# Value bias folded into the projection's bias, VectorE's chains in steps, and sixteen-bit transposes moved from TensorE to DMA

## The chip, the cores and the metric

The kernel runs on one core of a Trainium2 chip. The core has TensorE (PE, which has a second row for its weight loads), VectorE (DVE), ScalarE (ACT), GpSimd (POOL) and SyncE (SP, which here does nothing but issue DMAs), each with its own instruction queue worked off in order, and 16 DMA engines. Engines wait for each other through semaphores. The metric is the time of one execution on the device in microseconds, as a median.

## The reference, cut to what matters

Sixty-four sequences of 128 tokens with 128 features pass through four layers, each on a layer-normalised input and added to its input. The second operand of the two attentions is a context of 120 tokens.

```
def _L0_xattn_ref(x, ctx, Wq, bq, Wkv, bkv, Wproj, bproj, gq, gk):
    q = rms_norm((x @ Wq + bq).reshape(B, S, 16, 8), gq).transpose(0, 2, 1, 3)
    kv = (ctx @ Wkv + bkv).reshape(B, Sc, 2, 16, 8)
    k = rms_norm(kv[:, :, 0], gk).transpose(0, 2, 1, 3)
    v = kv[:, :, 1].transpose(0, 2, 1, 3)
    attn = softmax(einsum('bhsd,bhtd->bhst', q, k) / sqrt(8))
    out = einsum('bhst,bhtd->bhsd', attn, v) ...
    return out @ Wproj + bproj

def _L0_ffn_ref(x, w1, conv_w, conv_b, w2):          # 128 -> 512 -> 128
    h = silu(depthwise_conv1d(bit_linear(x, w1), conv_w, conv_b))
    return bit_linear(h, w2)                          # activations rounded to integers of -128..127 per row

x = x + _L0_xattn_ref(_layernorm(x), ctx, ...)
x = x + _L0_ffn_ref(_layernorm(x), ...)
x = x + _L1_xattn_ref(_layernorm(x), ctx, ...)        # one head of width 128
x = x + _L1_ffn_ref(_layernorm(x), ...)               # 8 experts of width 256; every token weighted by its gate
```

A row of `attn` sums to one, so a bias on the values comes out of the attention unchanged: `(attn @ (v + b)) @ Wproj + bproj` is `(attn @ v) @ Wproj + (b @ Wproj + bproj)`.

## The kernel before

The 64 sequences are cut into 16 groups of 4 (`GB`). A group passes through five stages: N (first layer norm, projections of Q, K and V, the RMS norms), A (attention of 16 heads, output projection), B (quantised feed-forward with the convolution), D (second attention, last layer norm, gate) and C (experts). They form a software pipeline: in one period stage N works on group i, A on i-1, B on i-2, D on i-3 and C on i-4. Twelve of the periods have all five stages; before them four fill the pipeline, and four empty it behind them.

Inside a period the order on each engine is a string of the table `TURNS`, one letter a step: the engine takes the next step of stage n, a, b, d or c as the string says. The stages' step lists are `n_steps` to `c_steps`. SP alone has its order written out, in its `body`.

The places that the change touches:

- Stage N, step `qkv`: V's projection lands in PSUM, and VectorE adds the bias `bv_s` in four instructions into `v_st` (L1037). Step `rms`: a chain of small VectorE instructions (`rsqrt`, L956 to L962), each of which waits for the one before it by a semaphore (`Chain.link`). Step `qkht`: TensorE transposes `q_hi` and `k_hi` (L492, L495), and ScalarE copies both to `qkht` (L745). From K's part SP issues 16 small DMAs, one a head, into the block-diagonal `kbd` (L413), after the last `max` step of the group ahead.
- Stage A: step `max` (L508) multiplies Q with `kbd` for four heads, VectorE takes the maxima (L1073); 16 such steps a group share one PSUM bank. Step `stacks` (four a group) transposes Q's stack (L518) and K's stack (L520) on TensorE, and ScalarE copies both to `st_t` (L752). `scores` (L532) multiplies them, ScalarE takes the exponentials (L756), `values` is L543.
- Stage B: step `quant` rounds the normalised input to integers (L1098 to L1107). Step `h2t` (four a group) transposes the hidden activations back (L590), VectorE finds each row's scale by a chain of four instructions (L1131 to L1134), ScalarE rounds (`hr`, L780); step `hit` transposes the integers on TensorE (L596) and ScalarE copies them from PSUM (L784); both steps use PSUM bank `pb`. `fc2` (L603) needs all four; L1136 forms its scales.
- Stage C: 16 units of three half-precision matmuls for `pg`, three for `pu`, and four for `py` (L697).

## Time and profile before

| | |
|---|---|
| median of 3 runs | 1278.15 us (1277.8 to 1279.9) |
| profiled execution | 1278.19 us |
| its span, first to last instruction | 1276.3 us |
| busy: PE, DVE, ACT, POOL | 1156.3, 1044.5, 865.6, 699.2 us |
| share of the span | 91%, 82%, 68%, 55% |
| mean granted TensorE clock | 0.951 of full |
| queue q1 (SP's DMAs): share of 16 engines' span | 8.4% |

Busy time counts stretches in which at least one instruction of the engine runs. TensorE's matmuls overlap: the next one starts before the one ahead has ended, so a group's array time is better read from the distance between starts. "Idle before" is time in which an engine stood still ahead of the group's instructions, with what released it. A row of stretches gives its bounds, its length, then the busy time of PE, PEld, DVE, ACT and POOL with the number of instructions in brackets, the granted TensorE clock as a share of full, the DMA engines' mean busy share and GB/s. SPq is the time that SP's queue spends to issue a DMA.

### The profile page before, as it was taken

How to read it: one execution, taken by the hardware profiler on the slowest of the kernel's cores; microseconds unless marked ns; L12 is line 12 of the kernel's file. 1: busy time of each engine (PE TensorE's matmuls, PEld its weight loads, DVE VectorE, ACT ScalarE, POOL GpSimd, SP SyncE). 2: the span in 40 equal slices, each digit the busy share in tenths (PEclk: the TensorE clock that was granted, in tenths of full speed). 3: DMA queues.
4: the chain of work that ended last, by engine and by line, in shares of the span. 5: the costliest groups of instructions: out<-in, count | busy, mean ns of one | idle time of the engine just before them, and what ended most of it. 6: DMA issues, size and time to landing. Idle time of an engine off the chain costs nothing.

```text
span 1276.3 us, 27899 instructions
## 1 busy us (share of the span) xinstructions
PE 1156.3 (91%) x10338; PEld 833.9 (65%) x10338; DVE 1044.5 (82%) x2837; ACT 865.6 (68%) x1684; POOL 699.2 (55%) x827
## 2 busy tenths in 40 slices
PE   1567578999999999999999999999999998999998
PEld 1344445675767677676767676776757676766775
DVE  3667877989889898989899898989898898768653
ACT  0335455786868686777868676877868685866665
POOL 3202122666464757566574747566664647455775
PEclk9656879999999999999999999999999999999999
DMA  6000001001010101001010101001010101000000
GB/s 198 21 10 12 12 25 29 17 4 43 10 37 17 38 17 37 18 5 43 10 36 18 37 17 37 18 21 33 4 44 9 38 2 37 17 10 17 10 9 9
DMA packets 63847, 32.69 MB, mean 26 GB/s; under 512 B 29281, under 2 KB 63073, under 8 KB 63329
## 3 DMA queue, kind: packets, MB, share of 16 engines
q1 hardware_dynamic: 61696, 26.83, 8.4%
q10 hardware_dynamic: 2016, 4.08, 0.9%
q8 instruction: 84, 1.38, 0.5%
q14 instruction: 51, 0.41, 0.1%
HBM read 24.73 MB, written 4.19 MB: 23 GB/s over the span
## 4 chain that ended last, share of the span: by engine, by line
PE 78%; DVE 10%; POOL 6%; ACT 3%; issue 2%; DMA 1%; SPq 0%; POOLq 0%; DVEq 0%; ACTq 0%
PE py L697 16%; PE pa L543 5%; PE pa L508 4%; PE pg L687 3%; PE pu L687 3%; PE pg L688 3%; PE pg L689 3%; PE pu L688 3%; PE pu L689 3%; PE pa L532 3%; POOL xn L856 2%; PE pa L550 2%; PE pb L590 2%; PE pb L596 2%; PE pa L697 2%
## 5 line engine op out<-in xcount | busy, mean ns | idle before, releaser
L895 POOL TENSOR_TENSOR moe<-moe 128x512 f32<-128x512 f32 x256 | 331.1, 1295 | 293.3 <-DVE moe L1194 179.0
L697 PE MATMUL py<-wd_s,moe 128*128 128x128 f32 x1856 | 250.7, 280 | 0.2
L697 PEld LDWEIGHTS py<-wd_s,moe 128*128 128x128 f32 x1856 | 232.9, 192 | 19.9 <-issue 4.4
L1073 DVE TENSOR_REDUCE q_st<-pa 128x4 f16<-128x480 f32 x256 | 168.4, 658 | 42.1 <-PE pa L508 40.2
L1194 DVE SCALAR_TENSOR_TENSOR moe<-tg,pg 128x512 f32<-128x512 f32 x232 | 157.8, 680 | 49.0 <-ACT tg L818 46.7
L818 ACT ACTIVATE tg<-pg 128x512 f32<-128x512 f32 x232 | 140.2, 604 | 75.2 <-PE pg L689 74.3
L756 ACT ACTIVATE probs<-pa 120x512 f32<-120x512 f32 x256 | 138.9, 598 | 49.4 <-PE pa L532 46.9
L832 ACT ACTIVATE moe<-pu 128x512 f32<-128x512 f32 x232 | 139.2, 600 | 15.9 <-PE pu L689 13.9
L508 PE MATMUL pa<-kbd,qkht 128*128 128x480 f16 x256 | 101.3, 396 | 24.5 <-DVE q_st L1073 19.5
L856 POOL TENSOR_SCALAR xn<-x,lnm,lnr 128x128 f32<-128x128 f32 x192 | 90.0, 481 | 5.2
L687 PE MATMUL pg<-x4h,wg_h 128*128 128x512 f16 x232 | 88.9, 383 | 3.7 <-DVE moe L1194 0.2
L687 PE MATMUL pu<-x4h,wu_h 128*128 128x512 f16 x232 | 88.3, 381 | 0.0
L688 PE MATMUL pg<-x4l,wg_h 128*128 128x512 f16 x232 | 88.3, 380 | 0.0
L688 PE MATMUL pu<-x4l,wu_h 128*128 128x512 f16 x232 | 88.2, 380 | 0.0
L689 PE MATMUL pg<-x4h,wg_l 128*128 128x512 f16 x232 | 88.2, 380 | 0.0
L689 PE MATMUL pu<-x4h,wu_l 128*128 128x512 f16 x232 | 88.0, 379 | 0.0
L850 POOL TENSOR_SCALAR lnv<-mv 128x4 f32<-128x4 f32 x64 | 16.8, 262 | 129.8 <-DVE mv L975 127.0
L752 ACT ACTIVATE st_t<-pa 128x992 f16<-128x992 f16 x64 | 64.0, 1000 | 28.5 <-PE pa L520 28.5
L532 PEld LDWEIGHTS pa<-st_t 32*120 32x120 f16 x1024 | 40.2, 134 | 59.7 <-ACT probs L756 22.4
L532 PE MATMUL pa<-st_t 32*120 32x128 f16 x1024 | 58.1, 234 | 19.4 <-ACT st_t L752 10.2
L543 PE MATMUL pa<-probs,v_st 120*9 120x128 f32 x2048 | 74.9, 289 | 0.3
L872 POOL TENSOR_SCALAR q_st<-q_hi 128x1024 f16<-128x1024 f16 x16 | 18.3, 1142 | 102.8 <-DVE q_hi L1060 102.8
(200 smaller groups left out, 2743.8 us busy)
## 6 DMA issues: line engine op xcount, KB each, us to landing
xin<-in_x SPq DMA_DIRECT2D x16, 256.0 KB, 2.8
xres<-in_x SPq DMA_DIRECT2D x16, 256.0 KB, 3.0
kbd<-qkht SPq DMA_DIRECT2D x256, 7.5 KB
out_x<-acc SPq DMA_DIRECT2D x16, 256.0 KB, 4.2
ctxt_a<-in_ctx_t SPq DMA_DIRECT2D x16, 240.0 KB, 2.7
ctxt_b<-in_ctx_t SPq DMA_DIRECT2D x16, 240.0 KB, 3.4
ctxn_b<-in_ctx SPq DMA_DIRECT2D x16, 240.0 KB, 4.1
wd_s<-in_wd ACTq DMA_DIRECT2D x1, 1024.0 KB, 8.4
```

Of the source, the lines that this page charges most:

```text
L508: pe.matmul(pa[:, BM, 0:4 * SC], qkht2[:, g % 2, t * S:(t + 1) * S], kbd[:, t, 4 * c:4 * c + 4, :], start=True, stop=True).then_inc(max_ps ...
L543: mm = pe.matmul(pa[32 * n:32 * n + HD + 1, BO, i * S:(i + 1) * S], v_st[0:SC, t, HQ * n + i, :], probs[0:SC, i, n, :], start=True, stop=True)
L687: pe.matmul(o[:, :], w_hi[:, us], x4h[:, :], start=True, stop=False)
L688: pe.matmul(o[:, :], w_hi[:, us], x4l[:, :], start=False, stop=False)
L689: pe.matmul(o[:, :], w_lo[:, us], x4h[:, :], start=False, stop=True).then_inc(done.sem, 1)
L697: mm = pe.matmul(moe_y(g, e)[:, j, :], hu[:, u % 3, j * S:(j + 1) * S], wd_s[:, u, :], start=(half == 0 and j == 0), stop=(half == 1), ski ...
L756: act.activation(probs[0:SC, i, :, :], pa[0:SC, i % 2, :], ACT.Exp).then_inc(p_done.sem, 1)
L818: act.activation(tg[:, u % 2, :], moe_bank("g", g, u)[:, :], ACT.Tanh, scale=0.5 / WSCALE).then_inc(tg_done.sem, 1)
L832: act.activation(us[:, u % 3, :], moe_bank("u", g, u)[:, :], ACT.Copy, scale=0.5 / WSCALE ** 2).then_inc(us_done.sem, 1)
L895: pool.tensor_tensor(hu[:, u % 3, :], gw[:, u % 3, :], us[:, u % 3, :], ALU.mult)\
L1073: dve.tensor_reduce(q_st[:, t, 4 * c:4 * c + 4, 3 * HD], pa[:, BM, 0:4 * SC].rearrange("p (h k) -> p h k", h=4), AX.X, ALU.max, negate=Tru ...
L1194: dve.scalar_tensor_tensor(out=gw[:, u % 3, :], in0=tg[:, u % 2, :], scalar=1.0, in1=moe_bank("g", g, u)[:, :], op0=ALU.add, op1=ALU.mult) ...
```

## The change

Three edits.

1. The value bias. `bv_s` no longer goes onto the values. Once, at the start, TensorE transposes it, multiplies it with `wp_s`, and VectorE adds the row to `bp_s`. The values are copied from PSUM by one ScalarE instruction a group instead of four on VectorE.
2. VectorE's chains. `link` is divided into `mark` (raise the semaphore) and `meet` (wait for it). `split` divides the steps `ln1`, `rms`, `ln2`, `quant`, `turn`, `h2t`, `ln3`, `s1`, `p1n`, `ln4` and `gate` at these points, so that the table may set steps of other stages between mark and meet. `quant` loses two instructions, and the scale of `fc2` is formed in `h2t`'s last step, a row of 128x1 each, in place of a product there and of L1136.
3. Transposes by DMA. `k_hi` to `kht`, `q_hi` to `qht`, K's whole stack `k_st` to `ks_t` (16 blocks of 128x128 in one DMA) and the integers `hq` to `hi_t` (four DMAs of 4 blocks a group) are transposed by `dma_start_transpose` from SP, seven DMAs and 40 blocks a group. TensorE's L492, L495, L520 and L596 go, and ScalarE's copy of `qkht`; `st_t` is 512 columns wide instead of 992. `hit` on ScalarE now reads `hr` in SBUF and writes `hq`. `kbd` is loaded in two halves, each of 16 DMAs of half the size: the first half behind `hit`'s DMAs, the second behind the last `max` of the group ahead. `k_st` is single, `ks_t` double.

SP's order is now a string of the table as well, and all strings were written anew.

```
-BANK = {"xn1t": S0, "q": S1, "k": S0, "v": S1, "qkht": S0, "d": S1}
+BANK = {"xn1t": S0, "q": S1, "k": S0, "v": S1, "d": S1}
...
-        "nab": "abaaaabaanaaabaanbabbaabbbaaaabaabbababababanbaaabbaaaaaaaababanbbnaanban",
+        "nab": ("abbaanabbaabbbnabaaabbnaabbbbnanabbnaabaaanabaababaanbbnbnnabnaaabanababbnanbbbbaabbbnaaaabaaaaa"
+                "baan"),
...
+        split = {"ln1": ["ln1", "ln1_mv"], "rms": [("rms", i) for i in range(10)], "ln2": ["ln2", "ln2_mv"],
+                 "quant": [("quant", i) for i in range(5)], "ln3": ["ln3", "ln3_mv"], "ln4": ["ln4", "ln4_mv"],
+                 "s1": ["s1", "nmax"], "p1n": ["rl", "p1n"], "gate": [("gate", i) for i in range(5)]}
+        for t in range(GB):
+            split[("turn", t)] = [("rden", t), ("turn", t)]
+            split[("h2t", t)] = [("h2t", t), ("clip", t), ("scale", t)]
...
+            def load_kbd(g, half):
+                part = slice(2 * half, 2 * half + 2)
+                if later(g):
+                    sp.wait_ge(max_ps.sem, max_ps.at(g - 1, 4 * (2 * half + 2)))
+                for h in range(H):
+                    rows = slice(h * HD, (h + 1) * HD)
+                    sp.dma_start(kbd[rows, part, h, :], kht[rows, part, 0:SC]).then_inc(kbd_in[half][h // HQ].sem, 16)
...
+                    sp.dma_start_transpose(kht[:, :, :], heads(k_hi)).then_inc(kht_in.sem, 16)
...
+                    sp.dma_start_transpose(qht2[:, g % 2, :, :], heads(q_hi)).then_inc(qht_in.sem, 16)
+                    sp.wait_ge(dup_done.sem, dup_done.at(g, 2))
+                    sp.wait_ge(kl_done.sem, kl_done.at(g))
+                    if g >= 2:
+                        sp.wait_ge(s_ps.sem, s_ps.at(g - 2, 2 * GB))
+                    sp.dma_start_transpose(ks_t2[:, g % 2, :, :, :].rearrange("p t n s -> p (t n) s"),
+                                           k_st[:, :, :, :].rearrange("p t h d -> p (t h d)")).then_inc(ks_in.sem, 16)
...
+                    sp.dma_start_transpose(hi_t[:, t, :, :], hq[:, t % 2, :]).then_inc(hit_in[t % 2].sem, 16)
...
+                    pe.transpose(pb[:, 128:256], bv_s[:, :], id_f[:, :]).then_inc(bvt_ps.sem, 1)
+                    pe.matmul(pb[:, 256:384], bvt[:, :], wp_s[:, :], start=True, stop=True)
...
-                    for n in range(NQ):
-                        mm = pe.transpose(pm16[:, NQ * S + n * SC:NQ * S + (n + 1) * SC],
-                                          k_st[0:SC, t, HQ * n:HQ * n + HQ, :], id_h[0:SC, 0:SC])
...
-                elif name == "hit":
-                    pe.wait_ge(hr_done.sem, hr_done.at(g, t + 1))
-                    take(PB, hit_done, g, t + 1)
-                    for k in range(KB):
-                        mm = pe.transpose(pb[:, k * S:(k + 1) * S], hr[:, t % 2, k * 128:(k + 1) * 128], id_f[:, :])
-                    mm.then_inc(hit_ps.sem, 1)
                 elif name == "fc2":
-                    pe.wait_ge(hit_done.sem, hit_done.at(g, GB))
+                    for part in hit_in:
+                        pe.wait_ge(part.sem, part.at(g, 8 * GB))
...
+                    act.wait_ge(v_ps.sem, v_ps.at(g))
+                    act.activation(v_st2[0:SC, g % 2, :, :, 0:HD].rearrange("p t h d -> p (t h) d"),
+                                   bank("v")[0:SC, :].rearrange("p (h d) -> p h d", d=HD), ACT.Copy).then_inc(v_done.sem, 1)
...
-                    act.activation(st_t[:, :], pm16[:, 0:NQ * (S + SC)], ACT.Copy).then_inc(st_done.sem, 1)
+                    act.activation(st_t[:, :], pa[:, BM, :].bitcast(F16)[:, 0:NQ * S], ACT.Copy).then_inc(st_done.sem, 1)
...
-                    act.wait_ge(hit_ps.sem, hit_ps.at(g, t + 1))
-                    act.activation(hi_t[:, t, :, :], pb[:, :], ACT.Identity, bias=unmagic[:, 0:1])\
-                       .then_inc(hit_done.sem, 1)
+                    act.wait_ge(hr_done.sem, hr_done.at(g, t + 1))
+                    if t >= 2:
+                        act.wait_ge(hit_in[t % 2].sem, hit_in[t % 2].at(g, 16 * (t // 2)))
+                    elif later(g):
+                        act.wait_ge(hit_in[t].sem, hit_in[t].at(g - 1, 8 * GB))
+                    act.activation(hq[:, t % 2, :], hr[:, t % 2, :], ACT.Identity, bias=unmagic[:, 0:1])\
+                       .then_inc(hq_done.sem, 1)
...
-                    cb.link(dve.tensor_scalar(inv2[:, :], am2[:, :], wmean[:, 1:2], 1.0 / 127.0, ALU.mult, ALU.mult))
+                    cb.meet()
```

SyncE in a full period, before. In brackets is what the first DMA of a row waits for; `kbd` is the block-diagonal K, `8x4x120` one head's rows of four sequences.

```order
L403 DMA xin<-in_x 128x4x128 [waits xn1_done]
L405 DMA ctxt_a<-in_ctx_t 128x4x120 [waits v_ps]
L413 DMA kbd<-qkht 8x4x120 [waits max_ps,qkht_done]
L413 DMA kbd<-qkht 8x4x120 x15
L418 DMA xres<-in_x 128x4x128 [waits xres_b_done]
L421 DMA ctxt_b<-in_ctx_t 128x4x120 [waits oc_ps]
L422 DMA ctxn_b<-in_ctx 120x4x128
L425 DMA out_x<-acc 128x4x128 [waits sum_done]
```

And now, from the `hit` DMA of the first sequence to the second half of `kbd`.

```order
L483 DMA_TRANSPOSE hi_t<-hq 128x4x128 [waits fc2_ps,hq_done]
L451 DMA_TRANSPOSE kht<-k_hi 128x4x128 [waits kbd10_in,kbd03_in,kbd11_in,kbd02_in,kbd12_in,kbd01_in,kbd13_in,kbd00_in,kh_done]
L483 DMA_TRANSPOSE hi_t<-hq 128x4x128 [waits hq_done]
L454 DMA_TRANSPOSE qht<-q_hi 128x4x128 [waits q_hi_done]
L459 DMA_TRANSPOSE ks_t<-k_st 128x16x128 [waits s_ps,kl_done,dup_done]
L483 DMA_TRANSPOSE hi_t<-hq 128x4x128 [waits hq_done] x2
L437 DMA kbd<-kht 8x2x120 [waits max_ps,kht_in]
L437 DMA kbd<-kht 8x2x120 x15
L475 DMA xres<-in_x 128x4x128 [waits xres_b_done]
L494 DMA out_x<-acc 128x4x128 [waits sum_done]
L437 DMA kbd<-kht 8x2x120 [waits max_ps]
L437 DMA kbd<-kht 8x2x120 x15
```

The last two `hit` DMAs now stand behind the one for K's stack, and the first half of `kbd` behind them.

TensorE around `fc2` (L603) in a full period, before: the last `hit` is L596.

```order
L596 MATMUL pb<-id_f,hr 128x128 [waits hr_done]
L596 MATMUL pb<-id_f,hr 128x128 x3
L687 MATMUL pu<-x4h,wu_h 128x512 [waits us_done]
L688 MATMUL pu<-x4l,wu_h 128x512
L689 MATMUL pu<-x4h,wu_l 128x512
L697 MATMUL py<-wd_s,moe 128x128 [waits hu_done]
L697 MATMUL py<-wd_s,moe 128x128 x3
L603 MATMUL pb<-w_i,hi_t 128x128 [waits hit_done]
L603 MATMUL pb<-w_i,hi_t 128x128 x15
L556 MATMUL pa<-id_f,o_n 128x128 [waits st_done,on_done]
L556 MATMUL pa<-id_f,o_n 128x128 x3
L668 MATMUL pa<-gate_h,x4h 128x8 [waits x4l_done]
```

And now, where `fc2` is L649.

```order
L714 MATMUL pa<-gate_h,x4h 128x8
L715 MATMUL pa<-gate_l,x4h 128x8
L716 MATMUL pa<-gate_h,x4l 128x8
L649 MATMUL pb<-w_i,hi_t 128x128 [waits hr_done,hit1_in,hit0_in]
L649 MATMUL pb<-w_i,hi_t 128x128 x15
L743 MATMUL py<-wd_s,moe 128x128 [waits hu_done,side_done]
L743 MATMUL py<-wd_s,moe 128x128 x3
L743 MATMUL py<-wd_s,moe 128x128 [waits hu_done]
L743 MATMUL py<-wd_s,moe 128x128 x3
L615 MATMUL pa<-wp_s,on_t 128x128 [waits on_done,ont_done]
```

`fc2` has moved behind the gate's products and waits for two DMA semaphores; the last `h2t` transposes (L641) stand 45 rows further up.

VectorE in `rms`, before: the chain stands in one piece.

```order
L1048 TENSOR_SCALAR ms<-ms 128x128 [waits link_n]
L956 TENSOR_SCALAR rr<-ms 128x128 [waits link_n]
L957 TENSOR_TENSOR root<-ms,rr 128x128 [waits link_n]
L959 SCALAR_TENSOR_TENSOR nt<-root,rr 128x128 [waits link_n]
L961 SCALAR_TENSOR_TENSOR root<-nt,root 128x128 [waits link_n]
```

And now, with maxima (`q_st`), an expert's product (`moe`) and a SiLU (`h`) between its links.

```order
L1113 TENSOR_SCALAR ms<-ms 128x128 [waits link_n]
L1020 TENSOR_SCALAR rr<-ms 128x128 [waits link_n]
L1144 TENSOR_REDUCE q_st<-pa 128x4 [waits max_ps]
L1022 TENSOR_TENSOR root<-ms,rr 128x128 [waits link_n]
L1024 SCALAR_TENSOR_TENSOR nt<-root,rr 128x128 [waits link_n]
L1296 SCALAR_TENSOR_TENSOR moe<-tg,pg 128x512 [waits tg_done]
L1207 SCALAR_TENSOR_TENSOR h<-th,cv 128x512 [waits th_done,cv_done]
L1026 SCALAR_TENSOR_TENSOR root<-nt,root 128x128 [waits link_n]
```

## Rows read from the trace of the kernel before

**Rows 1.** Busy time of each engine in four stretches; the last is eleven full periods.
```profile
36.20:82.10 45.90, 29.45 (x238) 18.84 (x239) 24.56 (x56) 18.35 (x26) 8.01 (x11) 0.57 0.06 15
205.70:279.60 73.90, 70.46 (x686) 50.26 (x684) 64.60 (x186) 55.22 (x107) 39.13 (x52) 1.00 0.08 20
1059.40:1130.00 70.60, 66.92 (x578) 48.58 (x576) 54.83 (x143) 49.40 (x99) 36.58 (x41) 0.95 0.10 25
279.60:1059.40 779.80, 761.71 (x7108) 556.02 (x7107) 701.48 (x1937) 587.41 (x1156) 479.68 (x562) 1.00 0.10 24
```

**Rows 2.** SP's timeline, start and length: the kbd loads at both ends.
```profile
279.60 11.64 SPq L413 DMA_DIRECT2D kbd<-qkht  x16
...
1059.40 11.64 SPq L413 DMA_DIRECT2D kbd<-qkht  x16
```

**Rows 3.** TensorE's waits from 279.6 to 1059.4: us, times, longest.
```profile
PE pa L508 <- DVE q_st L1073: 6.2, 22, 0.4
PE pb L574 <- DVE xq L1107: 5.1, 11, 0.8
```

**Rows 4.** TensorE's groups that go: count, busy us, mean ns, idle before.
```profile
L596 PE MATMUL pb<-id_f,hr 128*128 128x128 f32 x256 | 38.8, 274 | 2.2 <-ACT hr L780 1.9
L520 PE MATMUL pa<-id_h,k_st 120*128 120x120 f16 x256 | 25.2, 223 | 0.0
L492 PE MATMUL pa<-id_h,q_hi 128*128 128x128 f16 x64 | 7.0, 238 | 7.9 <-DVE q_hi L1060 7.9
L495 PE MATMUL pa<-id_h,k_hi 120*128 120x120 f16 x64 | 6.7, 232 | 0.0
```

**Rows 5.** TensorE's timeline in one full period, start and length.
```profile
565.55 0.60 PE L596 MATMUL pb<-id_f,hr 128*128 128x128 f32 x4
565.99 0.38 PE L687 MATMUL pu<-x4h,wu_h 128*128 128x512 f16 x1
...
577.35 0.36 PE L508 MATMUL pa<-kbd,qkht 128*128 128x480 f16 x1
...
578.88 0.38 PE L520 MATMUL pa<-id_h,k_st 120*128 120x120 f16 x4
579.09 1.11 PE L697 MATMUL py<-wd_s,moe 128*128 128x128 f32 x8
```

**Rows 6.** VectorE's groups that go or shrink.
```profile
L1037 DVE TENSOR_TENSOR v_st<-pa,bv_s 120x128 f32<-120x128 f32 x64 | 14.2, 284 | 5.9 <-PE pa L484 5.9
L1136 DVE TENSOR_SCALAR inv<-am,wmean 128x4 f32<-128x4 f32 x16 | 11.6, 727 | 0.0
L1134 DVE TENSOR_SCALAR sc<-sc 128x1 f32<-128x1 f32 x64 | 9.9, 154 | 2.2
L1101 DVE TENSOR_SCALAR inv<-am 128x4 f32<-128x4 f32 x16 | 2.7, 170 | 0.6
```

**Rows 7.** ScalarE's groups that go, shrink or resemble what comes.
```profile
L752 ACT ACTIVATE st_t<-pa 128x992 f16<-128x992 f16 x64 | 64.0, 1000 | 28.5 <-PE pa L520 28.5
L745 ACT ACTIVATE qkht<-pa 128x992 f16<-128x992 f16 x16 | 16.0, 997 | 3.9 <-PE pa L495 3.9
L784 ACT ACTIVATE hi_t<-pb,unmagic 128x512 bf16<-128x512 f32 x64 | 44.0, 688 | 17.9 <-PE pb L596 17.9
L809 ACT ACTIVATE x4h<-pa 128x512 f16<-128x512 f32 x16 | 9.5, 596 | 5.3 <-PE pa L662 5.3
L742 ACT ACTIVATE k_hi<-kb 120x512 f16<-120x512 f32 x16 | 10.2, 638 | 6.9 <-DVE kb L1055 6.9
```

**Rows 8.** SP's timeline in one full period, start and length.
```profile
527.40 0.37 SPq L403 DMA_DIRECT2D xin<-in_x  x1
...
563.07 11.97 SPq L413 DMA_DIRECT2D kbd<-qkht  x16
```

**Rows 9.** DMA issues: count, KB each, median us from issue to landing.
```profile
xin<-in_x SPq DMA_DIRECT2D x16, 256.0 KB, 2.8
```

**Rows 10.** ScalarE's timeline: the last hr of a group.
```profile
563.89 0.80 ACT L780 ACTIVATE hr<-pb,magic,sc 128x512 f32<-128x512 f32 x1
```

More of the change, by code:

```diff
@@ L257, in build_program @@
         dup_done = signal("dup_done", 2)
-        qkht_ps, qkht_done = signal("qkht_ps"), signal("qkht_done")
-        kbd_in = [signal(f"kbd{c}_in", 16 * HQ) for c in range(4)]
+        kht_in, qht_in, ks_in = signal("kht_in", 16), signal("qht_in", 16), signal("ks_in", 16)
+        kbd_in = [[signal(f"kbd{half}{c}_in", 16 * HQ) for c in range(4)] for half in range(2)]
         max_ps, max_done = signal("max_ps", 4 * GB), signal("max_done", 4 * GB)
@@ L277, in build_program @@
         hr_done = signal("hr_done", GB)
-        hit_ps, hit_done = signal("hit_ps", GB), signal("hit_done", GB)
+        hq_done, hit_in = signal("hq_done", GB), [signal(f"hit{i}_in", 8 * GB) for i in range(2)]
         fc2_ps, x2_done = signal("fc2_ps"), signal("x2_done")
@@ new lines, in do_a, with do_b @@
+            def do_a(step, g):
+                name, t, c = named(step)
+                if step == ("max", 0, 0) and later(g):
+                    load_kbd(g, 1)
+                elif name == "ont" and g < NG - 1:
+                    sp.wait_ge(xres_b_done.sem, xres_b_done.at(g))
+                    sp.dma_start(xres[:, :, :], x_g[g + 1]).then_inc(xres_in.sem, 16)
+            def do_b(step, g):
+                name, t, c = named(step)
+                if name == "hit":
+                    sp.wait_ge(hq_done.sem, hq_done.at(g, t + 1))
+                    if t == 0 and later(g):
+                        sp.wait_ge(fc2_ps.sem, fc2_ps.at(g - 1))
+                    sp.dma_start_transpose(hi_t[:, t, :, :], hq[:, t % 2, :]).then_inc(hit_in[t % 2].sem, 16)
@@ new lines, in do_d, with do_c @@
+            def do_d(step, g):
+                if step == "oc" and g < NG - 1:
+                    sp.wait_ge(oc_ps.sem, oc_ps.at(g))
+                    sp.dma_start(ctxt_b[:, :, :], ctxt_g[g + 1]).then_inc(ctxb_in.sem, 16)
+                    sp.dma_start(ctxn_b[0:SC, :, :], ctx_g[g + 1]).then_inc(ctxb_in.sem, 16)
+            def do_c(part, g):
+                if part == ("d", NU - 1):
+                    sp.wait_ge(sum_done.sem, sum_done.at(g, len(SIDE)))
+                    sp.dma_start(out_g[g], acc2[:, :, :]).then_inc(out_done.sem, 16)
@@ L439, in _, with idle @@
+            def idle(step, g):
+                pass
+            periods(sp, lambda n, a, b, d, c: run_turns("sp", n, a, b, d, c, idle, do_n, do_a, do_b, do_d, do_c))
             sp.wait_ge(out_done.sem, out_done.at(NG - 1, 16))
@@ L531, in do_a @@
                             r = slice(32 * i, 32 * i + 32)
-                            mm = pe.matmul(pa[0:SC, i % 2, n * S:(n + 1) * S],
-                                           st_t[r, NQ * S + n * SC:NQ * S + (n + 1) * SC],
-                                           st_t[r, n * S:(n + 1) * S], start=True, stop=True)
+                            mm = pe.matmul(pa[:, i % 2, n * S:(n + 1) * S], ks_t[r, n, :], qs_t[r, n, :],
+                                           start=True, stop=True)
                     mm.then_inc(s_ps.sem, 1)
@@ L1009, in do_w @@
                     dve.wait_ge(wint_done.sem, 1)
[L1010 removed]
+                elif step == "gate_w":
                     dve.wait_ge(gate_hi.sem, 1)
@@ L1034, in do_n @@
                        .then_inc(kb_done.sem, 1)
-                    dve.wait_ge(v_ps.sem, v_ps.at(g))
-                    for j in range(GB):
-                        ins = dve.tensor_tensor(v_st[0:SC, j, :, 0:HD],
-                                                bank("v")[0:SC, j * D:(j + 1) * D].rearrange("p (h d) -> p h d", h=H),
-                                                bv_s[0:SC, :].rearrange("p (h d) -> p h d", h=H), ALU.add)
-                    ins.then_inc(v_done.sem, 1)
-                elif name == "rms":
+                elif name == "rms" and t == 0:
                     dve.wait_ge(qk_sq.sem, qk_sq.at(g, 1))
```

399 lines of the change are left out of this document (226 added, 173 removed).

## The prediction

> **What bounds the kernel now.** I read the busy time by stretch first, then SP's timeline for the length of a period, then TensorE's waits, and then the groups that the change takes away.
>
> The start of the kbd loads gives the period: from 279.60 to 1059.40 us lie eleven full periods, 70.9 us each [rows 2]. There are twelve full periods, so two thirds of the time is twelve times this number. In these eleven periods TensorE is busy 761.71 of 779.80 us, 69.2 a period; VectorE 701.48, 63.8 a period; ScalarE 53.4, GpSimd 43.6 [rows 1]. TensorE's clock is at 1.00 there, its upper level of 2.4 GHz. TensorE stands still for little more than a microsecond a period, and then on VectorE: 6.2 us in all on a maximum, 5.1 on the quantised input [rows 3]. So TensorE sets the period and VectorE, 5.4 us behind it, is the next one. What leaves TensorE counts, until VectorE is the bound.
>
> The filling stage is another matter: from 36.2 to 82.1 TensorE is busy 29.45 of 45.9 us at a clock of 0.57, mostly the lower level of 1.2 GHz [rows 1]. There the chain through one group decides, not anyone's busy time.
>
> **TensorE.** Four groups go: L596 38.8 us busy, L520 25.2, L492 7.0, L495 6.7 [rows 4], together 77.7, or 4.86 us for each of 16 groups. But busy time includes a matmul's end, which lies under the next one. By distance between starts four transposes of L596 hold the array from 565.55 to 565.99, 0.44 us, and four of L520 from 578.88 to 579.09, 0.21 us [rows 5]. A group has four blocks of L596 (1.76), four of L520 (0.84) and one each of L492 and L495, taken like L520 (0.42): 3.0 us. The truth for the period lies between 3.0 and 4.86: the array is relieved by 3.0, and each removed block also takes a hand-over with it (stacks no longer outgrow their PSUM copy, `hit` no longer needs bank pb between two `h2t`). The scores' stationary operand is 128 instead of 120 wide, which I cost at nothing, as the moving side keeps 128 columns. The two matmuls of the bias run once.
>
> **VectorE.** Gone are the four additions of the value bias (14.2 us busy and 5.9 of idle ahead of them), L1136 (11.6), and in `quant` L1101 (2.7) and its like L1102, taken at the same [rows 6]: 14.2 + 5.9 + 11.6 + 5.4 = 37.1, or 2.3 us a group. The product L1134 (154 ns) gives way to a row of `inv2` of the same shape, nothing gained [rows 6]. Splitting the chains removes no work. The gaps in front of a linked instruction are small, 0.6 us for the 16 of L1101, so 0.04 us each [rows 6]; some forty links a group make 1.6 us that other steps can now fill, and a maximum that TensorE waits for no longer stands behind a whole chain. VectorE's need falls from 63.8 to about 61.5.
>
> **ScalarE.** `st_t` falls from 1000 ns to that of a half-precision copy of 512 columns, 596: 64 times 0.40 is 25.9 us. The copy of `qkht`, 16.0 us, goes; the copy of the values comes, 16 times about 0.6, 9.6 us. `hit` reads SBUF, 638 instead of 688 ns, 3.2 us [rows 7]. Net 35.5 us, 2.2 a group, from an engine with 17 us a period to spare: worth nothing by itself, except that scores wait for `st_t` for 0.4 us less, four times a group.
>
> **SP and the DMAs.** No row shows a transposing DMA. Before, 16 kbd loads hold SP's queue for 11.97 us, 0.75 each, while a load of 256 KB takes 0.37 [rows 8] and lands 2.8 us after its issue [rows 9]. Now there are 32 kbd loads of half the size and seven transposes, 40 blocks of 128x128. Bounds for a kbd load: 0.37 (halved) and 0.75; 12 to 24 us of queue a period. Bounds for a transpose: from below, one plain issue of 0.37 each, 2.6 us a period; from above the kbd price, which is 0.75 for 32 runs (8 rows of four sequences), so 3.0 us for a block's 128 rows and 120 us a period. These ends are far apart; I take the lower, because a transpose reads and writes whole 128-partition tiles as `xin` does, and kbd's eight-partition form is what is peculiar about kbd. With it SP's queue needs at most 24 + 3 + 2 = 29 of 67 us.
>
> The Trainium skill speaks with two voices here. "Advanced Engine Details and Errata", section X-Bar Transpose (TRN2), says that transposing DMAs are as fast as regular ones; by that the lower bound holds. "VectorE: DVE Perf Modes", section The three transpose paths, gives 1309 ns for one 128x128 block by DMA; an estimate from it is 40 times 1.31, 52 us a period, which is the second rival below. No run here shows either yet.
>
> **The sum.** A full period falls by 3.0 to 4.86 on TensorE; VectorE follows by 2.3 and has room. I take 3.6, the relieved array and a third of the difference: 70.9 to 67.3. Twelve periods: 43 us. Behind them, in 217 us from 1059.4 to the end, one group's K stacks (0.84) and two groups' `hit` (3.5) go: 4 us. In front, four groups need 9 us less of VectorE, and their TensorE work is at half clock, but the first group's chain exchanges 2 us of transposes and ScalarE copy for a landing of 2.8; I take 5 off, with bounds of 15 off and 10 on. In all 52 from the profiled execution's 1278.19 (the median of the runs is 1278.15, so nothing is to be added): 1226 us.
>
> **Rivals.**
>
> Tighter than forecast (A+). The split chains let maxima and quantisation come in time and the period falls to TensorE's whole busy difference and its waits of about 1: 70.9 - 4.9 - 1.0 = 65, hence 12 x 5.9 = 71, with 15 at the ends 86: 1192. For it: each of the PSUM hand-overs shortens. Against: VectorE would be busy 61.5 of 65, 95%, and was at 90% before.
>
> A new wait behind SP (B). The last `hit` DMAs stand behind K's stack, and kbd's first half behind them. In the trace the last `hr` ends at 564.7 [rows 10]; with `hq` at 0.64 and an issue the kbd loads begin at about 565.9. At 0.75 each the sixteenth is issued at 577.9 and lands at 580.7, while the fourth maximum of the next group starts at 577.35 [rows 5]: late by 3.4 us each period, which gives back nearly all: 1278 - 12 x 0.2 - 9 = 1267. At 0.37 each it lands at 574.6 and costs nothing. `fc2` can wait there too, if K's stack blocks the queue.
>
> Slower: the transposes fill the queue (C). The place is SP's queue and the DMA engines; SP needs 24 + 2 us besides, so a block may cost (67.3 - 26) / 40 = 1.03 us, and from there on the queue sets the period. At 1.31 a block the period is 26 + 52 = 78 us, 7.5 above before: 1278 + 90 = 1368, less if kbd's loads are cheap: at 0.37 the period is 66 and nothing is lost. So about 1290 to 1370. For it: no transposing DMA has been seen, and seven of them share one in-order queue with loads that others wait for. Against: the DMA engines are busy for a tenth of a full period [rows 1].
>
> The change does nothing: TensorE's relief is eaten by VectorE's order, within 0.2% (about what can be told from no change, 2.6 us).
>
> **Chances.** Forecast 0.48; A+ 0.17; B 0.14, mostly faster; nothing 0.03; C 0.15; a clock that falls below its upper level in full periods because TensorE is idle more often 0.03, slower as well. Hence faster 0.78, same 0.04, slower 0.18. The likeliest case's own range is 1205 to 1250; to leave no more than 2 in 10 outside, the range takes in A+ and B: 1188 to 1278.
>
> **What would show it.** Right: periods (kbd's first halves) 67.3 apart; TensorE's busy time down by 50 to 78 us in all, VectorE's by 31; the DMA queue's share up by a few per cent; issues of transposes under 1 us. B: TensorE's L561 or L649 waiting for a DMA two or three microseconds each period. C: SP's queue without gaps, ScalarE waiting for `hit_in`. A+: VectorE above 93% in full periods. Wrong would be the forecast if periods shrank by less than 2 us without a wait on a DMA: then VectorE's order, not TensorE's work, had set them.

## The result and the profile after

| | before | changed |
|---|---|---|
| first comparison | 1278.24 us (1277.8 to 1279.9, 4 runs) | 1242.97 us (1241.2 to 1243.6, 4 runs) |
| second comparison | 1279.31 us (1278.6 to 1281.5, 7 runs) | 1240.73 us (1239.3 to 1241.9, 4 runs) |
| profiled span | 1276.3 us | 1239.2 us |

The ratio is 0.972 (95% interval 0.9703 to 0.9736), and 0.9693 (0.9678 to 0.9707) when repeated on the chip of a later comparison. The forecast was 1226: right in direction and in what sets a period, 17 us too low, because the relief of a full period was sized too large.

The page of the changed kernel gives these busy times and this share for SP's queue:

```profile
PE 1100.0 (89%) x9701; PEld 775.9 (63%) x9701; DVE 991.8 (80%) x2728; ACT 825.6 (67%) x1685; POOL 680.8 (55%) x827
q1 hardware_dynamic: 149248, 47.82, 18.0%
```

TensorE is down by 56.3 us, VectorE by 52.7, ScalarE by 40.0. The queue's share went from 8.4% to 18.0%. The stretches, with the columns of [rows 1]; the last is eleven full periods, as there, and the one ahead of it a single one of them:

```profile
38.99:82.12 43.13, 25.98 (x208) 15.43 (x209) 23.21 (x52) 16.73 (x26) 7.21 (x10) 0.54 0.20 37
82.12:145.45 63.33, 43.28 (x373) 25.98 (x372) 44.93 (x108) 31.03 (x53) 10.34 (x17) 0.61 0.17 34
207.68:277.38 69.70, 65.70 (x596) 46.69 (x589) 58.02 (x164) 50.01 (x102) 38.54 (x51) 0.96 0.19 41
487.35:555.38 68.03, 65.41 (x608) 46.83 (x607) 60.11 (x169) 50.72 (x106) 42.08 (x52) 1.00 0.21 45
277.38:1033.44 756.06, 721.94 (x6671) 515.47 (x6669) 667.78 (x1861) 558.46 (x1156) 462.61 (x562) 1.00 0.21 44
```

SP's timeline, start and length, as [rows 2]: kbd's first halves.

```profile
207.68 11.65 SPq L437 DMA_DIRECT2D kbd<-kht  x16
...
277.38 11.65 SPq L437 DMA_DIRECT2D kbd<-kht  x16
...
1032.67 11.65 SPq L437 DMA_DIRECT2D kbd<-kht  x16
```

From 277.38 to 1032.67 are eleven periods of 68.66 us on average, where [rows 2] has 70.89. Six of them are 68.03 or 68.04 long, two 70.2 and 71.1, and the rest 68.3 to 68.9. The whole difference of the two spans, 37.1 us, divides like this (before, the row that answers to 207.68 stands at 205.74):

| stretch | before | after | difference | forecast |
|---|---|---|---|---|
| to the first full period | 205.74 | 207.68 | +1.9 | -5 |
| the first full period | 73.86 | 69.70 | -4.2 | -3.6 |
| eleven full periods | 779.80 | 755.29 | -24.5 | -39.6 |
| to the end | 216.9 | 206.5 | -10.4 | -4 |

So the error lies in the full periods (15 us) and in the front (7), and 6 of it is given back behind them.

TensorE's waits from 277.4 to 1033, as [rows 3] (us in all, times, longest):

```profile
PE pg L733 <- DVE moe L1296: 14.5, 11, 1.3
PE pa L561 <- DVE q_st L1144: 10.7, 11, 1.0
PE pb L625 <- DVE xn L1188: 3.6, 4, 1.4
PE pa L570 <- DVE q_st L1144: 3.4, 11, 0.3
PE pa L561 <- DMA kbd<-kht: 1.4, 4, 0.6
```

A regular period waits three times on VectorE: 1.32 (the gate product), 0.98 and 0.31 us (maxima), 2.6 in all. 65.4 busy and 2.6 waiting make 68.0. Before, TensorE stood still for 1.64 us a period (779.80 less 761.71, over eleven), 1.4 of it waiting on VectorE: the two rows of [rows 3] and a third one,

```profile
PE pa L518 <- DVE q_st L1073: 3.8, 11, 0.5
```

The two rarer rows above, of 4 times each, belong to the long periods. Not all of a long period is waiting, though. In the longest one the granted clock of TensorE fell to its lower level of 1.2 GHz for 3.4 us. The row of the period, and that of the fall:

```profile
346.01:417.15 71.14, 67.02 (x608) 47.21 (x607) 61.93 (x169) 50.72 (x106) 41.77 (x52) 0.98 0.22 43
357.30:360.70 3.40, 3.14 (x8) 1.17 (x9) 2.29 (x9) 0.60 (x1) 3.08 (x7) 0.51 0.31 92
```

The fall begins at the end of two waits, of 1.31 and 0.97 us with 1.0 us of work between them. TensorE's work took 1.6 us more in this period than in a regular one (67.02 against 65.41), and the quantised input came 1.2 us late. Before the change none of the eleven periods has such a fall of the clock. The same two waits stand in the other ten periods without one, so what else it takes isn't shown; but it matters for the experiments below.

All three regular waits lie at the opening of a period. TensorE's timeline there, then VectorE's (start, length, in brackets the idle time ahead and what ended it):

```profile
562.81 0.37 PE L561 MATMUL pa<-kbd,qht 128*128 128x480 f16 x1
564.49 0.39 PE L733 MATMUL pg<-x4h,wg_h 128*128 128x512 f16 x1 [1.32 <-DVE moe L1296]
...
566.49 0.36 PE L561 MATMUL pa<-kbd,qht 128*128 128x480 f16 x1 [0.97 <-DVE q_st L1144]
```

```profile
561.86 0.68 DVE L1162 TENSOR_TENSOR x<-pa,xres_b 128x512 f32<-128x512 f32 x1
562.58 0.87 DVE L1032 BATCH_NORM_STATS2 stats<-x 128x6 f32<-128x128 f32 x4
563.48 0.38 DVE L1038 BATCH_NORM_AGGREGATE mv<-stats 128x2 f32<-128x6 f32 x4
563.78 0.66 DVE L1296 SCALAR_TENSOR_TENSOR moe<-tg,pg 128x512 f32<-128x512 f32 x1
564.35 0.66 DVE L1144 TENSOR_REDUCE q_st<-pa 128x4 f16<-128x480 f32 x1
564.92 0.86 DVE L1032 BATCH_NORM_STATS2 stats<-x 128x6 f32<-128x128 f32 x4
565.70 0.65 DVE L1144 TENSOR_REDUCE q_st<-pa 128x4 f16<-128x480 f32 x1
```

VectorE has no gap to speak of here: it is the bound of this stretch, though over the period it is busy for only 60.1 of 68.0. SP's timeline of the same place, as [rows 8]:

```profile
541.53 1.22 SPq L483 DMA_TRANSPOSE hi_t<-hq  x1
543.05 1.19 SPq L451 DMA_TRANSPOSE kht<-k_hi  x1
545.89 1.19 SPq L483 DMA_TRANSPOSE hi_t<-hq  x1
547.13 1.26 SPq L454 DMA_TRANSPOSE qht<-q_hi  x1
549.50 1.86 SPq L459 DMA_TRANSPOSE ks_t<-k_st  x1
551.41 3.87 SPq L483 DMA_TRANSPOSE hi_t<-hq  x2
555.38 11.64 SPq L437 DMA_DIRECT2D kbd<-kht  x16
```

A transposing DMA of four blocks holds SP for 1.2 us, the one of sixteen blocks for 1.6 to 1.9. A kbd load of half the size costs 0.73, as much as a whole one before (0.75). The queue is idle for half of the period, but its 14 us ahead of the kbd loads are nearly full. How close the loads come is seen at the fourth score, which waits with its weight load (PEld) in this period too:

```profile
568.15 0.10 PEld L561 LDWEIGHTS pa<-kbd,qht 128*128 128x128 f16 x1 [0.50 <-DMA kbd<-kht]
```

Transposes from issue to landing, as [rows 9] (columns: count, median us):

```profile
hi_t<-hq SPq DMA_TRANSPOSE x64, 2.4
ks_t<-k_st SPq DMA_TRANSPOSE x16, 4.1
```

### The profile page after: what moved, and what is told of

It reads as the page before. It is cut to its first block, busy times and chain, and to the rows that moved or that the text cites. A ratio compares the mean times of both kernels' runs of the same rounds, so it can differ in the third digit from the quotient of the medians.

```text
span 1239.2 us, 27099 instructions
## 1 busy us (share of the span) xinstructions
PE 1100.0 (89%) x9701; PEld 775.9 (63%) x9701; DVE 991.8 (80%) x2728; ACT 825.6 (67%) x1685; POOL 680.8 (55%) x827
## 4 chain that ended last, share of the span: by engine, by line
PE 74%; DVE 11%; SPq 5%; POOL 3%; ACT 3%; issue 2%; DMA 1%; POOLq 0%; DVEq 0%; ACTq 0%
PE py L743 15%; PE pa L594 5%; PE pa L561 4%; SPq L437 4%; PE pg L733 4%; PE pu L733 3%; PE pg L735 3%; PE pg L734 3%; PE pu L735 3%; PE pu L734 3%; PE pa L584 3%; PE pb L641 2%; PE pa L601 2%; DVE q_st L1144 2%; PE pa L743 2%
## 5 line engine op out<-in xcount | busy, mean ns | idle before, releaser
L951 POOL TENSOR_TENSOR moe<-moe 128x512 f32<-128x512 f32 x256 | 335.9, 1316 | 295.4 <-ACT moe L886 149.4
L561 PE MATMUL pa<-kbd,qht 128*128 128x480 f16 x256 | 102.1, 399 | 34.5 <-DVE q_st L1144 32.1
L910 POOL TENSOR_SCALAR xn<-x,lnm,lnr 128x128 f32<-128x128 f32 x192 | 87.0, 465 | 5.2
L802 ACT ACTIVATE st_t<-pa 128x512 f16<-128x512 f16 x64 | 38.3, 599 | 56.0 <-PE pa L570 55.9
L561 PEld LDWEIGHTS pa<-kbd,qht 128*128 128x128 f16 x256 | 25.4, 99 | 79.1 <-issue 46.4
L594 PEld LDWEIGHTS pa<-probs,v_st 120*9 120x9 f32 x2048 | 51.5, 96 | 32.3 <-issue 26.1
L584 PE MATMUL pa<-st_t,ks_t 32*128 32x128 f16 x1024 | 54.2, 228 | 15.5 <-ACT probs L806 8.6
```

Of the source, the lines that this page charges most:

```text
L561: pe.matmul(pa[:, BM, 0:4 * SC], qht2[:, g % 2, t, :], kbd[:, t, 4 * c:4 * c + 4, :], start=True, stop=True).then_inc(max_ps.sem, 1)
L594: mm = pe.matmul(pa[32 * n:32 * n + HD + 1, BO, i * S:(i + 1) * S], v_st[0:SC, t, HQ * n + i, :], probs[0:SC, i, n, :], start=True, stop=True)
L951: pool.tensor_tensor(hu[:, u % 3, :], gw[:, u % 3, :], us[:, u % 3, :], ALU.mult)\
```

## The experiments

All times are medians. "Ratio" is against the kernel before in the same comparison, whose median was 1278 to 1281 each time; one thousandth is 1.3 us. The changed kernel stands at 0.972 and 0.9693, so a difference of 3 to 4 us between two comparisons means nothing. The e-runs are set against 0.972, the others against 0.9693. Where a time is taken apart by periods, a period at full clock is one of the eleven whose granted clock is 1.00, and a fall is a short stretch at the lower level, as above; the changed kernel has one fall in eleven periods, and its repetition a2_again has one too. A trace is of one execution: of the slowest one in e3, e4, o2 and h2, of the fastest in e1, h1 and k2.

| run | time us | ratio (95% interval) |
|---|---|---|
| e1_h2t_twice | 1267.22 | 0.9916 (0.9894 to 0.9938) |
| e2_vbias_dve | 1269.54 | 0.9905 (0.9871 to 0.9940) |
| e3_kstack_pe | 1271.78 | 0.9930 (0.9904 to 0.9956) |
| e4_chains_whole | 1307.32 | 1.0218 (1.0193 to 1.0244) |
| a2_again | 1240.73 | 0.9693 (0.9678 to 0.9707) |
| h1_more_transposes | 1264.24 | 0.9873 (0.9851 to 0.9896) |
| k1_kbd_16_loads | 1239.43 | 0.9677 (0.9661 to 0.9693) |
| k2_kbd_first_heads | 1240.77 | 0.9703 (0.9686 to 0.9719) |
| h2_more_plain | 1245.21 | 0.9729 (0.9716 to 0.9742) |
| o1_turns | 1252.28 | 0.9791 (0.9774 to 0.9808) |
| o2_turns_kbd | 1258.05 | 0.9832 (0.9814 to 0.9849) |
| k3_both_kbd | 1239.27 | 0.9688 (0.9666 to 0.9710) |

**TensorE's work (e1_h2t_twice).** Each of the 16 transposes of `h2t` a group runs twice.

```
-                    for k in range(KB):
+                    for k in [*range(KB), *range(KB)]:
```

> The changed kernel with each of the four groups of hidden-activation transposes of a period done twice into the same PSUM bank: 4 x 0.44 = 1.76 us more array time a full period, nothing else. Theory (TensorE's array time still sets a full period, so what leaves it comes off the period one for one): periods of 69.8 instead of 68.0, about +21 us in twelve periods and +3 to +6 at the ends, 1265 to 1270. Rival (VectorE's order sets the period now): TensorE has slack, less than a third comes back, under 1251.

Four of them more hold the array 0.44 us, by start distances, so 1.76 us a group and 28 in all; the time rose by 0.0196 of 1278, 25 us. The nine periods at full clock are 69.8 to 69.95 us long, 1.8 to 1.9 more than 68.03; two more have a fall and take 72.4. TensorE's array time counts at its full price, and this is the core of the forecast.

**The value bias back on VectorE (e2_vbias_dve).** The four additions return, ScalarE's copy goes.

```
-                    act.activation(v_st2[...], bank("v")[...], ACT.Copy).then_inc(v_done.sem, 1)
+                    for j in range(GB):
+                        ins = dve.tensor_tensor(v_st[0:SC, j, :, 0:HD], bank("v")[...], bv_s[...], ALU.add)
```

> The changed kernel with the value bias added by VectorE in four instructions again (0.89 us and about 0.3 of waiting a period) and ScalarE's copy of the values (0.6) gone; bias row not added to the projection's. Theory (TensorE sets the period, VectorE has room): +0 to +6 us, 1243 to 1249. Rival (VectorE sets it): 12 x 1.2 = 14 us and more, 1257 or above.

24 us more, for 14.1 us of work and 6.1 of idle ahead of it in the whole run. By its time the rival held, but the trace gives another cause for most of it. Eight of the eleven periods have a fall of the clock, where the changed kernel has one. One of the eight, and one without:

```profile
283.46:354.86 71.40, 67.16 (x608) 47.15 (x607) 62.54 (x173) 50.42 (x105) 41.92 (x52) 0.98 0.19 43
852.56:921.29 68.73, 65.58 (x608) 46.86 (x607) 60.81 (x173) 50.40 (x105) 42.22 (x52) 1.00 0.22 45
```

The eight take 71.2 to 72.0 us, the three at full clock 68.7 to 69.0. So the addition itself costs 0.7 to 1.0 us a period, less than its 1.3, and the falls cost 2.5 us each, some 20 in all. That is a comparison of periods within one trace; no run takes the clock alone. The mean granted clocks agree: the execution with 0.939, the changed kernel's own value, took 1259.0 us, the other four with 0.925 to 0.930 took 1268.2 to 1271.5. Each of the eight begins within 0.4 us of the end of the 0.97 us that the third score waits for its maximum; why this version has so many isn't shown. The forecast had counted VectorE's relief as room only, worth nothing while TensorE is the bound; at full clock it is worth a part of its length.

**K's stacks back on TensorE (e3_kstack_pe).** The sixteen-block DMA goes; four transposes a `stacks` step and the 992-column copy return.

```
-                            mm = pe.matmul(pa[:, i % 2, n * S:(n + 1) * S], ks_t[r, n, :], qs_t[r, n, :],
+                            mm = pe.matmul(pa[0:SC, i % 2, n * S:(n + 1) * S],
+                                           st_t[r, NQ * S + n * SC:NQ * S + (n + 1) * SC],
+                                           st_t[r, n * S:(n + 1) * S], start=True, stop=True)
```

> The changed kernel with K's stacks transposed on TensorE again (16 blocks, 0.84 us of array a period), copied by ScalarE with Q's in one instruction of 992 columns (1.0 instead of 0.6 us), and K's stack double again; that DMA transpose is gone. Theory (one for one): 12 x 0.84 = 10 us, plus up to 0.4 us a stack where the scores wait for the copy: 1253 to 1268. Rival (the DMA costs about what it saves, through SP's queue and the wait for kbd behind it): within 3 us of the changed kernel.

27 us more, a little above the expected range. Six of the eleven periods have a fall and take 71.7 to 72.3 us. Of the five at full clock three take 69.4 to 69.8, 1.4 to 1.7 more than 68.03, and two have longer waits. The transposes' array time (0.84 a group, 13 us) explains half of the 27. ScalarE's copy is 0.4 us longer again, with the scores waiting for it four times a group; I had named that term and then priced it at nothing. The copy, the DMA and the falls were not tested apart.

**Chains not divided (e4_chains_whole).** Same instructions and same table, but VectorE takes all parts of a divided step at the place of its first.

```
+                if step in done:
+                    continue
+                parts = whole.get((stage, step), [step]) if engine == "dve" else [step]
+                for part in parts:
+                    do[stage](part, groups[stage])
+                    done.add(part)
```

> The changed kernel with VectorE's divided steps run whole where their first part stands: same instructions, same waits, other order, and an order string that was not made for it. Theory (dividing fills about forty gaps of 0.04 us and lets maxima through): +5 to +25 us, 1248 to 1268. Rival (dividing is what carries the gain): the whole 35 us and more are lost, 1278 or above. Rival (dividing is worth nothing): within 3 us of the changed kernel.

64 us more: all of the gain and 29 us besides. The table was made for divided steps, so this is no fair price of dividing alone. It shows that under an order that doesn't fit them the other parts of the change can be lost whole. Here too the clock has a share: ten of the eleven periods have a fall, and the one at full clock takes 72.3 us, 4.3 more than 68.03. VectorE's timeline of this run shows what a link costs. The second instruction waits for the first by a link; the fourth needs nothing of the third:

```profile
578.01 0.68 DVE L1223 TENSOR_REDUCE am<-pb 128x1 f32<-128x512 f32 x1
578.73 0.15 DVE L1226 TENSOR_SCALAR am<-am 128x1 f32<-128x1 f32 x1
...
583.24 0.68 DVE L1281 TENSOR_TENSOR x4l<-pa,x4h 128x512 f16<-128x512 f32 x1
583.84 0.68 DVE L1307 SCALAR_TENSOR_TENSOR moe<-tg,pg 128x512 f32<-128x512 f32 x1
```

and TensorE's the waits that follow from late maxima and products, the longest of them:

```profile
599.00 0.58 PE L581 MATMUL pa<-id_h,q_st 128*128 128x128 f16 x4 [2.33 <-DVE q_st L1155]
```

**SP's queue (a2_again, h1_more_transposes, h2_more_plain).** Three extra DMAs of 128 KB a period, once as transposes, once as plain copies; nobody reads them.

```
+                    if t < 3:
+                        ...
+                        sp.dma_start_transpose(spare[:, :, :], w1_i[:, :]).then_inc(spare_in.sem, 16)
```

> The changed kernel once more, on the chip and in the rounds of the three beside it, as their reference. Every theory expects 1243 us, within 4.

> Three more transposing DMAs of 4 blocks a period (into a spare tile, nobody reads it), each ahead of one of the first three of the FFN's integers: 3 x 1.2 = 3.6 us more of SP's queue a period, in the 14 us ahead of the next kbd loads, where the trace of the changed kernel shows gaps of 1.65 and 1.1 us. Theory 'the queue ahead of the kbd loads is full': the loads come 0.9 to 3.6 us later, TensorE had 0.5 to 1.2 us of weight loads waiting for them already, so 12 to 35 us longer in all, 1255 to 1278. Rival 'SP is busy for half of the period and the loads have room': within 4 us of the changed kernel, 1239 to 1247.

> The three extra DMAs of h1_more_transposes at the same places and of the same 128 KB, as plain copies. Their issue should cost SP 0.4 to 0.5 us each (the loads of x and of the context over 128 partitions take 0.37 to 0.52) in place of 1.2. Theory 'what costs is the time that SP is held up by issuing, in front of kbd's loads': 1.3 instead of 3.6 us a period, so 1242 to 1251. Rival 'what costs is one more transfer and its semaphore in the chain, whatever its kind': 1258 to 1268 as with the transposes.

The extra DMA's row in both, transposing first (ns min/median/max of the issue, and us from issue to landing):

```profile
L488 SPq DMA_TRANSPOSE spare<-w_i x48: 1188/1217/2430, 128.5 to 1166.8; - x48
...
DMA to landing us min/median/max: 2.4/2.5/4.9
```

```profile
L488 SPq DMA_DIRECT2D spare<-w_i x48: 465/535/560, 128.7 to 1152.4; - x48
...
DMA to landing us min/median/max: 2.0/2.1/4.1
```

3.65 us more of issuing a period made it 23 us longer, 1.6 us made it 4.6, and h2_more_plain comes from another comparison than its reference: against 0.972 its 4.6 would be 1.2, so it is not clear of nothing. Falls of the clock don't explain the 23 us: the first has two in eleven periods, the second three. The number of transfers and semaphores is the same in both, so it is not these. In the first, TensorE waits for kbd as rival B said,

```profile
PE pa L567 <- DMA kbd<-kht: 14.8, 14, 1.9
```

and for the quantised input oftener, 9.0 us in 8 times.

So the stretch of SP's queue ahead of kbd is a third resource at its limit, with little slack: 1.6 us a period cost at most 0.3, the next 2 cost more than half of their length. The two variants also differ in the time their data take on the DMA engines (below), so the issue alone is the likely cause, not a proven one.

**kbd's loads (k1_kbd_16_loads, k2_kbd_first_heads).**

```
-                part = slice(2 * half, 2 * half + 2)
+                part = slice(0, 4) if g < 2 else slice(2 * half, 2 * half + 2)
...
```

```
+                    if g >= 2:
+                        sp.wait_ge(kht_in.sem, kht_in.at(g, 16))
+                        sp.wait_ge(max_ps.sem, max_ps.at(g - 1, 8))
+                        for h in range(HQ):
+                            ...
+                            sp.dma_start(kbd[rows, 0:2, h, :], kht[rows, 0:2, 0:SC]).then_inc(kbd_in[0][0].sem, 16)
```

> For groups 0 and 1 kbd is loaded by 16 DMAs of 4 blocks instead of 32 of 2: a half costs SP the same 0.69 us as a whole would, so SP is done 11 us sooner in each of the two. Theory 'the front is set by SP's queue' (4% of the chain that ended last is this line, some 47 us, two runs of 23.5): 10 to 23 us less, 1220 to 1233. Rival 'the first score needs only the first loads, and the rest of the front has other limits': at most 4 us less, 1239 or more. If a load of double size costs double, nothing changes and the row shows 1.4 us each.

> From group 2 on, four of the 16 kbd loads that open a period are issued ahead of the transposes of K's stacks and of the last two integers, so that the last kbd load is out 2.8 us sooner and K's stacks 2.8 us later. Theory 'kbd comes just in time and makes the irregular periods (69 to 71 us instead of 68.0)': 3 to 10 us less, 1233 to 1240. Rival 'K's stacks and the integers are as tight': 5 to 30 us more. Third: VectorE's order sets the periods and nothing changes, within 3 us of 1243.

Eleven microseconds less of SP in each of two periods of the front gave 1.3 us (the intervals overlap), and the first full period begins at 205.75 instead of 207.7: SP's kbd loads of these two groups do not bound the front, though their line stood in the chain that ended last. The second changed nothing either, by its median. In its profile, the fastest of its executions, TensorE's waits for kbd and for the quantised input are gone, and from 277 to 1000 the three regular ones stand nearly alone (14.5, 10.7 and 3.6 us, and 0.8 for GpSimd). No period has a fall of the clock, and counted from one load of `xin` to the next they lie between 67.5 and 68.7 us. So the waits of the changed kernel's long periods go with where kbd's loads stand in the queue; but other executions of this version took up to 1242.2 us, and no gain can be claimed.

**The opening's order (o1_turns, o2_turns_kbd).** VectorE takes the first products and maxima ahead of the statistics' ends; TensorE takes the second up projection between two scores. The strings of full periods:

```
-        "nabdc": ("ccbbacaaccadcaca...   (TensorE)
+        "nabdc": ("ccbbacacacadcaca...
...
-        "nabdc": ("cbbccadacabcdbac...   (VectorE)
+        "nabdc": ("cbcabcacadbcdbac...
```

> The changed kernel with two strings of turns edited at the opening of a full period: VectorE takes the first two gate products and the first three score maxima ahead of the statistics' ends (0.8 us sooner), TensorE takes the second up projection between the second and third scores. Theory 'the regular period of 68 us is 65.4 us of TensorE's work and 2.6 us of waits at this opening (1.3 for the gate product, 1.0 and 0.3 for the maxima)': 0.7 to 1.5 us a period less over 12 periods, 1224 to 1236. Rival 'SP's queue, with kbd just in time, sets the period': the waits turn into waits for kbd and the time stays within 3 us of 1241. Third: LayerNorm's statistics come later and the conv-FFN's transposes wait for them: 1245 or more.

> The turns of o1_turns together with both edits of kbd's loads (16 loads of full size for groups 0 and 1; from group 2 on the loads of the first four heads ahead of the transposes of K's stacks). If the period's opening and SP's queue both bind, each hides what the other gives and only both together pay: 1215 to 1232, and at least 3 us below o1_turns. If VectorE's order alone sets the period, it is o1_turns less 1 to 2 us for the front. If the later statistics cost, 1243 or more.

Both lost, 12.5 and 18 us. In o1_turns the periods at full clock take 69.1 to 69.2 us instead of 68.03, and four with a fall 70.2 to 70.4; in o2_turns_kbd six have a fall. The first kernel's waits of TensorE:

```profile
PE pa L561 <- DMA kbd<-kht: 11.6, 12, 1.7
PE pa L570 <- DVE q_st L1144: 11.4, 11, 1.2
PE pg L733 <- DVE moe L1296: 10.2, 11, 0.9
PE pa L561 <- DVE q_st L1144: 2.0, 10, 0.2
```

The two waits that the edit aimed at did shrink, from 1.3 to 0.9 and from 1.0 to 0.2 us. In their place came one for kbd, up to 1.7, and one before L570, 1.2 instead of 0.3. With the later statistics GpSimd's input for the quantisation is late, VectorE stands still for it and the fourth maximum follows late. VectorE's timeline:

```profile
567.54 0.69 DVE L1175 TENSOR_REDUCE am<-xn 128x4 f32<-128x512 f32 x1 [0.52 <-POOL xn L910]
...
568.68 0.65 DVE L1144 TENSOR_REDUCE q_st<-pa 128x4 f16<-128x480 f32 x1
```

With kbd earlier as well (o2_turns_kbd) the wait for kbd is gone and the maxima take over whole:

```profile
PE pa L584 <- DVE q_st L1158: 23.9, 11, 2.2
```

**Both kbd edits (k3_both_kbd).**

> Both edits of kbd's loads without the new turns: the version that the experiments point to. Alone, the first left 1239.4 and the second 1240.8 (its best execution 1234.4, with every period at 68.2). If each frees its own place (the front, and the uneven periods), together 1233 to 1239, below the changed kernel's 1241 to 1243. If a period's start only shifts against VectorE's turns, 1239 to 1243 and no difference.

1239.3 us, ratio 0.9688: the same as the changed kernel within what can be measured. Its trace, of an execution of 1237.5 us, again has no fall in the eleven periods and no wait for kbd. No version of these is faster than it beyond doubt.

## Why the prediction came out as it did

**TensorE sets the period: right.** Its busy time fell by 56.3 us, within the 50 to 78 forecast. The array relief of 3.0 us a group by start distances is what the regular period shows, 70.87 to 68.03, 2.84. e1_h2t_twice put 1.76 us back and got 1.8 to 1.9 in a period at full clock.

**"The relieved array and a third of the difference", 3.6 us: this term failed.** The busy time fell by 3.8 a period (69.2 to 65.4), between the two bounds, but 1.0 us of that turned into waiting on VectorE at the opening (TensorE stands still for 2.6 us instead of 1.6), so the third was not had: 0.7 us a period, 8 us in eleven. The prediction had read "little more than a microsecond" of idle off two rows of waits; the stretch it quoted gives 1.64, and the relief could have been expected to meet the order of VectorE there. On top of it five periods are longer than 68.04, by 7 us together: 3.1 of it the period with the fall of the clock, the rest waits for the quantised input and for kbd. The mean relief was 2.2 instead of 3.6.

**A lower clock in full periods, chance 0.03: it happened, in small.** One fall in eleven periods, and a granted clock of 0.96 in the first full period, where the kernel before had 1.00. Its price, 3.1 us in the changed kernel and 2.5 in e2_vbias_dve (1.1 in o1_turns), stood in no term of the sum.

**VectorE's room: its size right by one measure, its worth wrong.** The sum over VectorE's groups fell from 1118.5 to 1088.5 us, 30 for the 31 forecast, but its busy time by 52.7. The rest is overlap. An instruction that waits for nothing starts before the end of the one ahead (0.60 us after the start of one of 0.68); a linked one starts after it (0.72, the rows of e4_chains_whole above). A link costs 0.12 us, not the 0.04 that I read from the idle column, because that column leaves the lost overlap out. VectorE's need per period is 60.1 to 60.7, not 61.5. Still the average said little: it is saturated in the ten microseconds at the opening of a period, and there o1_turns shows that a displacement costs (1.1 us a period at full clock). e2_vbias_dve shows room elsewhere: 1.3 us more of VectorE cost 0.7 to 1.0 at full clock, and the rest of its 24 us came with the clock.

**ScalarE: as forecast by its busy time** (40.0 for 35.5 us), less by the sum over its groups, which fell by 27.0: `hit` takes 745 ns, not 638, so it rose instead of shrinking, and the rest of the 40.0 is overlap. Its work was priced at nothing; that fits ScalarE being idle for 17 us of a period, but e3_kstack_pe leaves open whether the shorter `st_t` is worth something.

**SP and the DMAs: the direction right, the price wrong.** I took 0.37 us an issue for a transpose; it is 1.2. Halved kbd loads cost the upper bound, 0.73. The queue needs 23.3 + 8.8 + 2.8 = 35 us of a period instead of 29. The upper end, 3.0 us a block, was far off: 0.3 us of issue a block in the small ones and 0.1 in the large one.

The rule of the Trainium skill's "Advanced Engine Details and Errata", X-Bar Transpose (TRN2), that transposing DMAs are as fast as regular ones, comes near here for the landing only (2.5 us against 2.1 in h1_more_transposes and h2_more_plain), not for the issue (1.22 against 0.54) nor for the DMA engines' time (0.72 against 0.35, below). The 1309 ns for a 128x128 block of "VectorE: DVE Perf Modes", The three transpose paths, is no price of a block in a larger DMA: `ks_t` lands sixteen of them in 4.1 us.

**Rival C (transposes fill the queue): refuted** by SP's timeline, idle for half of the period. **Rival B (kbd behind the transposes): its mechanism is there, its size isn't.** It said 3.4 us late each period; only the weight load waits, 0.5 us in a regular one and up to 1.2 in a long one. B had taken 2.8 us for a kbd load's landing, from a load of 256 KB; the last of the sixteen is issued by 567.02 and its weight load starts at 568.15, so it takes 1.1. And the fourth score comes 12.8 us after the first load's issue, not 11.4. h1_more_transposes shows that B begins at once when the queue gets more. **A+ (the hand-overs shorten, waits vanish): half of it came true,** the busy time, and VectorE took it back at 88% of its time, not above 93%.

**The front: wrong by 7 us.** No gain came from 9 us less of VectorE. By the starts of the kbd loads, which no longer stand at quite the same place of TensorE's order, the first stretch is 2.8 us longer than before, with three transposes ahead of the first load. The next two are 2.8 and 2.5 us shorter. The one ahead of the first full period is 4.4 longer, before and now:

```profile
147.95:205.74 57.79, 37.70 (x312) 25.75 (x310) 43.97 (x116) 25.96 (x48) 15.47 (x26) 0.73 0.07 17
145.45:207.68 62.23, 42.19 (x361) 27.66 (x358) 44.36 (x127) 30.76 (x58) 17.30 (x30) 0.69 0.21 49
```

So the loss is in the last one, where also more of TensorE's work falls (361 instructions for 312), and where TensorE waits 3.1 and 4.1 us for two maxima; before it waited there 1.4 us at most for one, though 2.7 and 2.3 us for kbd and 3.2 for the quantised input. The clock over the front is lower, 0.67 instead of 0.72, but that doesn't look like the price: a2_again and h1_more_transposes, at 0.69 and 0.71, begin the first full period at 207.3, the changed kernel at 207.7. No run changes the order there, so the cause stays open. k1_kbd_16_loads excludes SP's loads of the first two groups.

**The end: 6 us better than forecast.** TensorE is busy for 194.7 instead of 204.2 us there. A part of the difference is work that only moved across the boundaries (8 fewer `py` matmuls here, 8 more in the first full period); no run takes the rest apart, and it stays open.

## To carry to other kernels

Price a removed instruction by the distance between starts, and then look at what stands ready at the places where the bounding engine already waits: relief turns into waits there. Where the trace gives a clock, compare periods at the same clock before a change is priced: in e2_vbias_dve 0.7 to 1.0 us a period was the edit and 2.5 us each of eight periods a fall of the clock. Shares over a period don't tell of room; the busiest ten microseconds do, and a queue that is idle for half of the time can be full just ahead of the load that matters. In a table tuned as a whole, parts cannot be priced by undoing one: here each undone part cost 24 to 64 us, together three times the gain, and a part of it came with the clock.
